# Exponentials three score banks at a time in the second attention of a gated decoder

## The reference, cut to what matters

```python
def _L1_xattn_ref(q, k, v):
    qh = q.reshape(B, h, d, Tq)      # 64 batches, 8 heads, 8 rows, 256 columns
    kh = k.reshape(B, h, d, Tk)
    vh = v.reshape(B, h, dv, Tk)
    qn = _l2norm(qh, axis=-2)
    kn = _l2norm(kh, axis=-2)
    qk = ALPHA * jnp.einsum('bhdq,bhdk->bhqk', qn, kn)
    sm = jax.nn.softmax(qk, axis=-1)
    out = jnp.einsum('bhqk,bhdk->bhdq', sm, vh)
    return out.reshape(B, Dv, Tq)
...
x = x + jnp.tanh(g_xattn[1]) * _L1_xattn_ref(_layernorm(x, axis=-1), ctx_2048, ctx_2048)
```

## Time and profile before

| what | value |
| --- | --- |
| median of three runs | 3785.6 us (3783.56 to 3797.69) |
| the profiled execution, its own time | 3776.57 us |
| its span in the profile | 3774.7 us |
| granted TensorE clock, mean over the span | 0.873 |
| TensorE busy over the whole span | 2875.6 us (76%) |
| ScalarE busy over the whole span | 1493.7 us (40%) |
| VectorE busy over the whole span | 2273.3 us (60%) |
| first and last start of an exponential of the second attention | 1606.1 and 1859.6 us |

### The profile page before, as it was taken

How to read it: one execution, slowest core, us unless ns; L and a number is a source line. 1 busy time by engine, 2 the same in 40 slices (tenths; PEclk the granted TensorE clock), 3 DMA queues, 4 the chain that set the end, 5 groups by cost and what they waited for, 6 DMA issues and landing times. The chain is left out here.

```text
span 3774.7 us, 60424 instructions
## 1 busy us (share of the span) xinstructions
PE 2875.6 (76%) x19922; PEld 1822.1 (48%) x19922; DVE 2273.3 (60%) x5171; ACT 1493.7 (40%) x3091; POOL 885.2 (23%) x1241
## 2 busy tenths in 40 slices
PE   5388885465899993399716599899979839999993
PEld 4233334222555552233303377444547638888782
DVE  7699983676677775633467788788869730000003
ACT  5277771254222225399614355222235302121110
POOL 3111110376233336211100033000023261111110
PEclk7599995798999995599857799999989859999996
DMA  8766633499222224478100153000034321111204
GB/s 262 176 118 118 121 90 134 159 367 359 88 82 80 80 75 170 114 134 118 26 24 0 45 168 104 2 1 1 1 96 141 102 83 55 46 59 48 84 27 134
DMA packets 261309, 386.20 MB, mean 102 GB/s; under 512 B 56321, under 2 KB 188654, under 8 KB 260768
## 3 DMA queue, kind: packets, MB, share of 16 engines
q1 hardware_dynamic: 234192, 312.76, 31.1%
q0 software_dynamic: 25152, 68.22, 5.2%
q10 hardware_dynamic: 1680, 1.57, 0.2%
HBM read 227.75 MB, written 160.24 MB: 103 GB/s over the span
## 5 line engine op out<-in xcount | busy, mean ns | idle before, releaser
L3022 POOL DMA_INDIRECT rows_out<-e_out,e_tr_dest x224 | 234.7, 1048 | 872.0 <-DVE e_out L3652 521.2
L1188 ACT ACTIVATE a_pt<-a_psS 128x512 f32<-128x512 f32 x512 | 277.5, 595 | 152.1 <-PE a_psS L1086 147.7
L3652 DVE COPY e_out<-e_psD 128x512 f32<-128x512 f32 x40 | 27.7, 692 | 491.8 <-PE e_psD L3620 491.7
L1210 DVE TENSOR_REDUCE a_mx_sb<-a_psM 128x4 f32<-128x1024 f32 x256 | 292.9, 1215 | 17.2 <-PE a_psM L1069 16.0
L3420 PE MATMUL e_psG<-e_wgu,e_yT 128*128 x576 | 275.1, 600 | 27.0 <-ACT e_yT L3448 24.4
L1100 PE MATMUL a_psV<-a_pt,a_vt 128*18 128x256 f32 x4096 | 291.4, 386 | 1.3 <-issue 0.8
L3620 PE MATMUL e_psD<-e_w,e_hT 128*128 128x256 f32 x1280 | 289.7, 386 | 0.0
L3609 PE MATMUL e_psH<-e_yT,e_w 128*128 128x256 f32 x1280 | 284.4, 381 | 1.6 <-issue 0.8
L3552 ACT ACTIVATE e_hT<-e_psH 128x512 f32<-128x512 f32 x160 | 95.5, 597 | 451.8 <-PE e_psH L3609 451.8
L3620 PEld LDWEIGHTS e_psD<-e_w,e_hT 128*128 128x128 f32 x1280 | 245.8, 195 | 32.8
L3609 PEld LDWEIGHTS e_psH<-e_yT,e_w 128*128 128x128 f32 x1280 | 244.5, 191 | 35.0 <-issue 2.1
(11 more groups left out here) (420 smaller groups left out, 5997.7 us busy)
## 6 DMA issues: line engine op xcount, KB each, us to landing
kbd<-e_bgu SPq DMA_DIRECT2D x64, 512.0 KB, 4.5
cr_kbd<-kbd SPq DMA_DIRECT2D x64, 512.0 KB, 3.4
rows_in<-zeros POOLq DMA_DIRECT2D x36, 522.0 KB, 6.5
e_xin<-rows_in SPq DMA_DIRECT2D x144, 128.0 KB
vbd<-e_bd SPq DMA_DIRECT2D x64, 272.0 KB, 4.2
cr_vbd<-vbd SPq DMA_DIRECT2D x64, 272.0 KB, 2.7
cq_rows<-rows_out SPq DMA_DIRECT2D x32, 512.0 KB, 5.8
e_w<-in_L_ffn_w_dram SPq DMA_DIRECT2D x16, 1024.0 KB, 7.6
```

Of the source, the lines that this page charges most:

```text
L1188: act.activation(pt[:, probs(t, h), b, :, :], psS[:, unit(t, h, b) % S_BANKS, :].rearrange("p (k c) -> p k c", k=KC), ACT.Exp, scale=scale ...
L1210: dve.tensor_reduce(mx[:, t % 2, :, h, :], psM[:, k % 2, :, :].rearrange("p b (f c) -> p b f c", f=2), AX_X, ALU.max).then_inc(ring_read, 1)
L3022: pool.indirect_dma_start(out=self.rows_out[0:limit, :], out_offset=bass.IndirectOffsetOnAxis(ap=self.dest[:, t:t + 1], axis=0), in_=rows, ...
```

## The change

ScalarE no longer takes one head at a time, but three units, over the borders of heads: units 0-2, 3-5, 6-8 and so on. Three banks are always banks 0-2 or 3-5 of psS and three neighbours among the 24 unit places of pt. It waits for the `st_done` of the last two units of the three, for the slots of all three, and raises `exp_done` by 3. The last call takes the two units that are left. With 512 units that makes 171 calls in place of 256. TensorE's program, its waits and its order are as before, and so is the first attention.

```diff
     S_BANKS = 3 if with_max else 6
+    EXP_UNITS = 3
     EXP_BUFS = 2 * HEADS if with_max else HEADS + HEADS // 2
...
-                for t in range(TILES):
+                def exp_units(first, last):
+                    for u in (last - 1, last):
+                        act.wait_ge(st_done[u % 2], u // 2 + 1)
+                    for u in range(first, last + 1):
+                        before = u // 2 - EXP_BUFS
+                        if before >= 0:
+                            act.wait_ge(pv_done, lump(before // HEADS, u % 2, before % HEADS // 4) + 1)
+                    count, at, bank = last + 1 - first, first % (2 * EXP_BUFS), first % S_BANKS
+                    act.activation(pt[:, :, :, :, :].rearrange("p e b k c -> p (e b) k c")[:, at:at + count, :, :],
+                                   psS[:, bank:bank + count, :].rearrange("p u (k c) -> p u k c", k=KC), ACT.Exp, scale=scale).then_inc(exp_done, count)
+
+                if not with_max:
+                    for first in range(0, PAIR * TILES, EXP_UNITS):
+                        exp_units(first, min(first + EXP_UNITS, PAIR * TILES) - 1)
+                for t in range(TILES if with_max else 0):
                     for h in range(HEADS):
...
-                        else:
-                            for b in range(2):
-                                act.wait_ge(st_done[b], HEADS * t + h + 1)
-                            probs_free(t, h, 1)
-                            first = unit(t, h, 0) % S_BANKS
-                            act.activation(pt[:, probs(t, h), :, :, :], psS[:, first:first + 2, :].rearrange("p b (k c) -> p b k c", k=KC),
-                                           ACT.Exp, scale=scale).then_inc(exp_done, 2)
```

## The result

The changed kernel takes 3834.59 us in the median of three runs (3834.57 to 3838.71), against 3785.6 before: 49.0 us more, ratio 1.0131 with the interval 1.0115 to 1.0147. The forecast was 3842 with the range 3826 to 3861.

What follows compares the result with a forecast made beforehand. TensorE and ScalarE were taken to bound the second attention together, about 7.55 us a tile each. Terms +53.9 (31 tiles), +2.4, +0.5 and -0.5 gave +56.3 us on the 3785.6 median: 3842 us, range 3826 to 3861.

Steps and rivals of the forecast that it cites:

- head 3j+1: Middle head of each three, in banks 2 and 3; its scores wait for exp_done 6j, making 9.28 us per eight heads.
- call B: Exponential call over banks 3 to 5, second of a round; put at 1.47 us to its end.
- call A: Exponential call over banks 0 to 2, first of a round; put at 1.37 us to the start of call B.
- plain round: Three heads, from one call A to the next, with two value heads or fewer; put at 3.48 us.
- step from scores to exponential: Time from the start of the awaited scores on TensorE to the start of call A; put at 0.60 us.
- straddling head: Same as head 3j+1: it lies across the border between banks 0 to 2 and banks 3 to 5.
- round with three value heads: Three heads all followed by value matmuls, so TensorE's own work sets the time; put at 3.93 us, two rounds in eight.
- first tile: Second attention's opening tile, no values, low clock: rounds of 3.64 us, eight heads 9.71 in place of 7.33, +2.4 us.
- first call of Exp: Start of the second attention's exponentials: it waits for a second head's scores, put at +0.5 us.
- The ring: Six psS score banks, only two three-bank calls; the rival claim that it costs nothing had a 3% chance.
- first rival: Second attention: both engines reach their own work, TensorE bounds at 7.54 us a tile, gain 9 us, 3777 us; chance 3%.
- third rival: TensorE's clock in the second attention might fall to 1.2 GHz; with a quarter of tiles +35 us, 3877; chance 5%.

Runs made afterwards that it cites:

- coupled kernel: Kernel before, two-bank calls kept, with only the changed kernel's dependence between scores and exponentials added by waits: 3849.59 us, ratio 1.0155.

## Why the prediction was right

**The sign and the mechanism.** The prediction put the whole loss on one step, head 3j+1 waiting for call B and call A waiting for head 3j+1. The chain is in the timeline as it was described; putting it alone into the kernel before brings the loss (62.6 us, some 54 without the falls of the clock), and issuing the scores so that no head lies across the border takes back 37 of 49 us.

**The size, 56.3 forecast, 49.0 measured.** The terms:

- The plain round was put at 3.48 us and takes 3.40 to 3.47, most often 3.40. Two parts of it were too large. The call was put at 1.468 by the line through three sizes and has a median of 1.450:

```profile
L1191 ACT ACTIVATE a_pt<-a_psS x171: 1033/1450/1452, 1615.0 to 1917.1; 128x1536 f32<-128x1536 f32 x170, 128x1024 f32<-128x1024 f32 x1
```

 The step from scores to exponential was put at 0.60, and it is 0.56 (1718.79 to 1719.35), so the idle time is 0.61 where 0.64 was said. The likely reason is only argued: the 0.60 had been read from a call that needs both batches of a head, while call A needs batch 0 alone of the straddling head. The coupled kernel, whose call needs both, shows 0.60 again (1703.52 to 1704.12).
- The round with three value heads was put at 3.93 and takes 3.94, two in eight, as counted. Eight rounds of the changed kernel, from 1701.23 to 1729.55, take 28.32 us, 9.44 a tile in place of 9.58: 31 x 0.14 = 4.3 us of the 7.3 that were too much.
- The first tile was put at 3.64 a round and takes 3.57, with 0.78 of idle time in the low clock; the first call of Exp came 2.41 us after the first scores, against 2.02 before, 0.4 where 0.5 was expected:

```profile
1612.58 1.46 PE L1087 MATMUL a_psS<-a_qa,a_ka 48*128 48x256 bf16 x12 [36.62 <-DMA a_ka<-n_pieces]
1614.99 2.79 ACT L1191 ACTIVATE a_pt<-a_psS 128x1536 f32<-128x1536 f32 x2
1618.56 2.79 ACT L1191 ACTIVATE a_pt<-a_psS 128x1536 f32<-128x1536 f32 x2 [0.78 <-PE a_psS L1087]
1622.13 2.79 ACT L1191 ACTIVATE a_pt<-a_psS 128x1536 f32<-128x1536 f32 x2 [0.78 <-PE a_psS L1087]
1624.18 1.91 PE L1101 MATMUL a_psV<-a_pt,a_vt 128*18 128x256 f32 x16
1626.75 2.92 ACT L1191 ACTIVATE a_pt<-a_psS 128x1536 f32<-128x1536 f32 x2 [1.82 <-PE a_psS L1087]
1630.85 2.79 ACT L1191 ACTIVATE a_pt<-a_psS 128x1536 f32<-128x1536 f32 x2 [1.19 <-PE a_psS L1087]
```

- The rest, some 2.7 us, is for the most part what the kernel before lost beyond its 7.84 us a tile. The prediction set 31 tiles of 7.84 against 31 new ones; the timeline of before shows more:

```profile
1617.97 1.02 ACT L1195 ACTIVATE a_pt<-a_psS 128x1024 f32<-128x1024 f32 x1 [1.16 <-PE a_psS L1086]
1619.33 1.02 ACT L1195 ACTIVATE a_pt<-a_psS 128x1024 f32<-128x1024 f32 x1 [0.34 <-PE a_psS L1086]
1620.65 7.55 ACT L1195 ACTIVATE a_pt<-a_psS 128x1024 f32<-128x1024 f32 x8 [0.29 <-PE a_psS L1086]
...
1685.71 1.77 PE L1100 MATMUL a_psV<-a_pt,a_vt 128*18 128x256 f32 x16
...
1762.54 1.02 ACT L1195 ACTIVATE a_pt<-a_psS 128x1024 f32<-128x1024 f32 x1 [0.29 <-PE a_psS L1086]
1763.88 0.59 PE L1086 MATMUL a_psS<-a_qa,a_ka 48*128 48x256 bf16 x7 [1.44 <-issue]
1764.43 6.77 ACT L1195 ACTIVATE a_pt<-a_psS 128x1024 f32<-128x1024 f32 x7 [0.87 <-PE a_psS L1086]
```

 Low-clock values in the first tile that has them cost waits of 0.44, 1.16 and 0.34 us beside the regular one of 0.29 at 1620.65, 1.94 more. The changed kernel pays for its own: its rounds from 1622.13 and from 1626.75 take 4.62 and 4.10 us, and the same two rounds of a later tile, from 1708.58 and 1712.01, take 3.43 and 3.94, so 1.35 more. And from 1620.65 to 1857.77 the kernel before has 30 tiles in 237.1 us, where 30 x 7.843 makes 235.3. Two tiles were disturbed, both at a granted clock of 1.00 and both by TensorE: in the one that starts at 1762.54 (1.1 us) it is idle for 1.44 us up to 1763.88, with nothing in the profile that it waits for, and in the other (0.7 us) sixteen value matmuls take 1.77 us at 1685.71 in place of 1.06. Why is not known. Together 1.94 - 1.35 + 1.8 = 2.4 us; some 0.3 stay unexplained.

**What it said would be seen.** 171 calls, 170 of 1536: yes. Some 85 waits of ScalarE and about 70 us: 84 and 64.2 us. A stage of 316 us: 314.4, and that this is so near is partly luck, since the prediction counted the stage before as 261 us and the same two marks that give 314.4 give 265.4 for it: the growth was put at 55 and is 49.0. ScalarE's busy time was to fall by 5 to 10 us and fell by 2.9. There the prediction used the spacing of calls back to back for all of them, while every second call now begins behind an idle time and has no call before it to overlap: 86 x 1.45 + 85 x 1.35 = 239.5. So even the saving that was the change's whole ground is mostly given back in the same engine.

**The rivals.** The ring didn't hide the wait. The bound of 7.54 us a tile that the first rival gave to TensorE was too high: the kernel before with values behind heads 0, 2, 3 and 4 takes 7.46. The clock stayed at 1.00 in the changed kernel in each stretch of 16 us from 1632 on, so the third rival is out for it. The Trainium skill, "TensorE: Matmul & The Clock Gate", section "A second HAM failure mode: psum-queue depth-cycling", has it that small idles between groups of matmuls that cycle through PSUM banks can make the clock swing. That swing is not seen in the changed kernel, but one like it is in the coupled kernel, whose waits look the same. What tells the two apart stays open, and so does whether the page's case is the one at work there. The Trainium skill, "ScalarE: Activation LUTs", section "What ACT_TABLE_LOAD costs", gives 186 + 0.833 x 1536 = 1466 ns for a call whose scale and bias are immediates, an estimate; the trace has 1450. The wide call did what the change said, 170 calls of 1536.

## What to carry to other kernels

A ring's worth is counted in calls of its reader, not in banks: three places of two banks overlapped, two places of three did so for long only where the writer filled exactly one place at a time, and even then the kernel was slower (the waits for slots of pt may have a share in that). Before a call is widened, ask which writes lie across the new border, since one of them puts both engines in a line, with two signals in each round. And where two engines are equally full, the order of the one's work in time can be worth more than fewer instructions on the other: here one value group moved by one head brought 8.1 us, and 85 calls fewer brought none.

## What was not expected of the hardware

- The granted clock of the coupled kernel falls to half for stretches of a few us, a mean of 0.89 over 16 us, with TensorE busy for 12.66 us of 16 and single waits of 1.44 us. The changed kernel has 12.60 of 16 and a wait of 1.45 us at 1.00. In these two kernels the busy share alone does not say whether the clock holds. The kernel before with values behind heads 0, 2, 3 and 4 has one such fall too, at 1690, behind an idle time of TensorE of 2.11 us.
- A call that begins behind an idle time of ScalarE and one that follows another have nearly the same duration, but the second starts 0.10 us before the first has ended: 2.80 us for two of 1.45. The way from the end of a call over the scores that waited for it to the start of the next call costs 0.61 us in the changed kernel at full clock and 0.78 at the low one, about half as much as a call. That holds both signals between the engines and the matmuls of the straddling head; the rows don't part them.
